# A sorting step beside block-softmax attention: its pieces placed anew over the slots

## What is computed

```
x = x + attn_b(layernorm(x), Wq, Wk, Wv, Wo)        # block softmax, keys in blocks of 64
xf = layernorm(layernorm(x)) * ln_g + ln_b
logits = xf @ router_w                              # [tokens, 8]
scores, idx = top_k(logits, 2); gate = softmax(scores)
out = sum over experts e of gates[:, e] * expert_e(xf)
```

## Time and profile before

| | us |
|---|---|
| median of 3 runs | 2684.78 (2684.75 to 2685.96) |
| profiled execution | 2703.54 |
| its span | 2701.7 |
| PE busy | 2364.6 (88%) |
| DVE busy | 2263.5 (84%) |
| ACT busy | 1622.9 (60%) |
| POOL busy | 1483.6 (55%) |

### The profile page before, as it was taken

How to read it: one execution, slowest core, us unless ns; L and a number is a source line. 1 busy time by engine, 2 the same in 40 slices (tenths; PEclk the granted TensorE clock), 3 DMA queues, 4 the chain that set the end, 5 groups by cost and what they waited for, 6 DMA issues and landing times. The chain is left out here.

```text
span 2701.7 us, 44016 instructions
## 1 busy us (share of the span) xinstructions
PE 2364.6 (88%) x15040; PEld 1796.7 (67%) x15040; DVE 2263.5 (84%) x4665; ACT 1622.9 (60%) x2803; POOL 1483.6 (55%) x1060
## 2 busy tenths in 40 slices
PE   6992179965899999999999999999999999929994
PEld 3552168853677777777777777777777777618883
DVE  5527557757999999999999999999999999737775
...
GB/s 97 157 152 65 42 161 186 195 129 151 110 110 88 102 127 79 98 133 87 69 78 92 68 74 72 87 59 74 84 90 59 74 95 53 14 34 182 189 191 158
DMA packets 171134, 281.22 MB, mean 104 GB/s; under 512 B 32892, under 2 KB 124674, under 8 KB 170912
## 3 DMA queue, kind: packets, MB, share of 16 engines
...
## 5 line engine op out<-in xcount | busy, mean ns | idle before, releaser
L1917 POOL TENSOR_TENSOR b_prob<-b_prob,b_weight 128x1024 f32<-128x1024 f32 x512 | 958.8, 1904 | 514.9 <-DVE b_weight L1877 514.5
L1847 DVE TENSOR_REDUCE b_bmax<-b_score 128x16 f32<-128x1024 f32 x512 | 620.4, 1212 | 38.7 <-PE b_score L1702 24.9
L1800 ACT ACTIVATE b_prob<-b_score,b_neg_m 128x1024 f32<-128x1024 f32 x512 | 582.5, 1138 | 96.1 <-DVE b_neg_m L1855 95.8
L1834 DVE TENSOR_REDUCE b_bsum<-b_prob 128x16 f32<-128x1024 f32 x512 | 605.6, 1202 | 0.0
L1786 ACT ACTIVATE b_pT<-b_turn 128x512 f32<-128x512 f32 x1024 | 561.3, 610 | 60.1 <-PE b_turn L1715 53.3
L1715 PE MATMUL b_turn<-ident,b_prob 128*128 128x128 f32 x4096 | 532.8, 273 | 3.1 <-ACT b_pT L1786 2.8
L1715 PEld LDWEIGHTS b_turn<-ident,b_prob 128*128 128x128 f32 x4096 | 478.7, 141 | 74.4 <-ACT b_pT L1786 3.2
L1702 PE MATMUL b_score<-b_KH,b_QS 128*128 128x512 f32 x1024 | 473.4, 462 | 26.1 <-ACT b_prob L1800 24.9
L1682 PE MATMUL b_acc<-b_pT,b_V 128*64 128x256 f32 x4096 | 470.3, 382 | 0.0
L1702 PE MATMUL b_score<-b_KL,b_QS 128*128 128x512 f32 x1024 | 405.1, 396 | 0.0
L1682 PEld LDWEIGHTS b_acc<-b_pT,b_V 128*64 128x64 f32 x4096 | 282.7, 137 | 151.1 <-issue 21.4
...
...
## 6 DMA issues: line engine op xcount, KB each, us to landing
...
b_KH<-b_k_high SPq DMA_DIRECT2D x128, 256.0 KB
b_KL<-b_k_low SPq DMA_DIRECT2D x128, 256.0 KB
...
```

Of the source, the lines that this page charges most:

```text
L1800: act.activation(prob[r % 4][k][:], score[k % 2][:], ACT.Exp, bias=neg_m[r % 2][:, k:k + 1]).then_inc(prob_ready, 1)
L1834: dve.tensor_reduce(bsum[r % 2][:, k, :], prob[r % 4][k][:].rearrange("p (n c) -> p n c", c=KV_BLOCK), AX, ALU.add).then_inc(sum_ready, 1)
L1847: maxima = chain.mark(dve.tensor_reduce(bmax[r % 2][:, k, :], score[k % 2][:].rearrange("p (n c) -> p n c", c=KV_BLOCK), AX, ALU.max))
L1917: pool.tensor_tensor(tile, tile, weight[r % 2][:, k, :].unsqueeze(2).to_broadcast([P, NB, KV_BLOCK]), ALU.mult).then_inc(scaled, 1)
```

## The change

`LateSort` is split into `Sorter` (the pieces) and `BesideSlots` (their places). It is built with `ways` = 1, so nothing is held twice. The inverse root is made another way: ScalarE takes `Sqrt` of the variance, VectorE its reciprocal, where ScalarE had taken Ln and Exp. What moves:

| piece | engine | `t` before | `t` now |
|---|---|---|---|
| reciprocal, square, fix / rest of the correction | DVE | - and 5 | 5 / 6 |
| normal rows | ACT | 6, 7 | 7, 8 |
| gain, shift | POOL | 8, 9 | 10, 11 |
| second statistics, aggregate, variance | DVE | 10 to 13 | 12 to 15 |
| second root, correction | ACT, DVE | 14, 15 | 16, 17 |
| choice of the two experts | DVE | 19 to 21 | 19 to 21, cut otherwise |
| counts | PE | 21, quarter 2 | 21, quarter 3 |
| places, slots | DVE | 23, 24 | 23, 24, 25 |
| scattering DMAs | POOL | 25 to 30: 3, 3, 2, 3, 3, 2 | 26 to 31: 4, 4, 1, 1, 4, 2 |

VectorE's pieces now stand at the end of quarter 2, but for the copies out of `misc` (logits at `t` 14 and 18, counts at 22), which stay at the end of quarter 0. For sequence 2 the last DMAs are 4, 4, 1, 1, 6.

```diff
-                        if k == PLACE_AT:
+                        if k == 0:
+                            late.vector_takes(dve, sl)
+                        if k == 2:
                             late.vector(dve, chain, sl, wo_taken)
...
-        if t == 8:
...
-        if t == 9:
...
-        if t in (25, 28):
...
-        if 25 <= t < 31:
-            k, third = divmod(t - 25, 3)
...
+        if t == 10:
+            s.pool_gain(pool, n)
+        if t == 11:
+            s.pool_shift(pool, n)
+        if t == 26:
+            s.pool_number(pool, n, 0)
+            s.pool_scatter(pool, n, 0, 0, 4)
+        if t == 27:
+            s.pool_scatter(pool, n, 0, 4, 8)
+        if t == 28:
+            s.pool_number(pool, n, 1)
+            s.pool_scatter(pool, n, 1, 0, 1)
+        if t == 29:
+            s.pool_scatter(pool, n, 1, 1, 2)
+        if t == 30:
+            s.pool_scatter(pool, n, 1, 2, 6 if n + 2 < BATCH else 8)
...
+    def inverse(self, dve, chain, n, which):
...
+        chain.link(dve.reciprocal(self.rstd[:], self.std[:]))
         chain.link(dve.tensor_tensor(self.square[:], self.rstd[:], self.rstd[:], ALU.mult))
         chain.link(dve.tensor_tensor(self.fix[:], self.square[:], self.var[:], ALU.mult))
+    def correct(self, dve, chain):
         chain.link(dve.tensor_scalar(self.square[:], self.fix[:], -0.5, 1.5, ALU.mult, ALU.add))
         chain.link(dve.tensor_tensor(self.rstd[:], self.rstd[:], self.square[:], ALU.mult))
         dve.scalar_tensor_tensor(self.bias[:], self.both[:, :, 0], -1.0, self.rstd[:], ALU.mult, ALU.mult).then_inc(self.biased, 1)
...
+        if t == 5:
+            s.inverse(dve, chain, n, 0)
+        if t == 6:
+            s.correct(dve, chain)
...
+        if t == 17:
+            s.inverse(dve, chain, n, 1)
+            s.correct(dve, chain)
         if t == 19:
+            s.best_of(dve, chain, n)
         if t == 20:
+            s.first_best(dve, chain)
+            s.pick_first(dve, chain)
         if t == 21:
+            s.second_of(dve, chain, n)
+            s.first_best(dve, chain)
+            s.pick_second(dve, chain)
         if t == 23:
+            s.tiles_before(dve, chain, n)
         if t == 24:
+            s.places(dve, chain, n)
+        if t == 25:
+            s.to_slots(dve, chain, n)
```

More of the change, by code:

```diff
@@ L835, in begin, with number, data, normal_rows @@
         self.slot_f = sb("slot_f", [P, 2, TPB])
[L836 to L848, removed]
+        self.slots = [sb(f"slots{i}", [P, 2, TPB], mybir.dt.uint32) for i in range(ways)]
+    LOADS = 5 * 16
+    def number(self, n):
+        return n
+    def data(self, n):
+        return self.rows[n % self.ways][:, :, 0:D]
+    def normal_rows(self, n):
+        return self.hat[:] if self.apart else self.data(n)
+    def loads(self, eng):
+        eng.wait_ge(self.loaded, 48)
     def sync(self, sp):
@@ new lines, in pool_scatter, with pool_end, turn @@
+    def pool_scatter(self, pool, n, k, first, end):
+        for i in range(first, end):
+            pool.indirect_dma_start(out=self.sorted_rows,
+                                    out_offset=bass.IndirectOffsetOnAxis(ap=self.slots[n % self.ways][:, k, i:i + 1], axis=0),
+                                    in_=self.rows[n % self.ways][:, i, :], in_offset=None).then_inc(self.moved, 16)
+    def pool_end(self, pool):
+        pool.wait_ge(self.moved, 32 * TPB * self.number(BATCH - 1))
+    def turn(self, pe, n, half, bank):
+        m = self.number(n)
+        if half == 0:
+            if self.apart:
+                pe.wait_ge(self.normal, m + 1)
+            else:
+                pe.wait_ge(self.xf_ready, m + 1)
+        for i in range(4):
+            last = pe.transpose(bank[:, i * P:(i + 1) * P], self.normal_rows(n)[:, 4 * half + i, :], self.ident[:])
+        last.then_inc(self.turned, 1)
@@ new lines, in scalar_z, with statistics @@
+    def scalar_z(self, act, n, half):
+        m = self.number(n)
+        if half == 0:
+            act.wait_ge(self.biased, 2 * m + 2)
+            if not self.apart:
+                act.wait_ge(self.turned, 2 * m + 2)
+        for i in range(4 * half, 4 * half + 4):
+            row = self.data(n)[:, i, :]
+            last = act.activation(row, row, ACT.Identity, scale=self.rstd[:, i:i + 1], bias=self.bias[:, i:i + 1])
+        if half:
+            last.then_inc(self.z_ready, 1)
+    def statistics(self, dve, chain, n, which, half):
+        if which and half == 0:
+            dve.wait_ge(self.xf_ready, self.number(n) + 1)
+        for i in range(4 * half, 4 * half + 4):
+            src = self.data(n)[:, i, :] if which else self.X[:, n * TPB + i, :]
+            last = dve.bn_stats(self.parts[:, i, :], src)
@@ L1406 @@
 CLEAR_IN = 12
-PLACE_AT = 0
 class Front:
```

390 lines of the change are left out of this document (216 added, 174 removed).

## The result

| | before | after |
|---|---|---|
| median | 2684.93 | 2746.89 |
| lowest to highest of 4 runs each | 2684.75 to 2685.96 | 2745.33 to 2747.46 |
| profiled execution | 2703.54 | 2747.46 |
| its span | 2701.7 | 2745.6 |

After takes 1.0229 times as long as before (95% interval 1.0211 to 1.0247), 62.0 us more; 2720 was predicted. No engine has much more work: this is the page's first part of after (busy time, share of the span, instructions), to be held against the earlier trace rows.

What follows compares the result with a forecast made beforehand. Slots are bound by a loop of weights, GpSimd's weighing and VectorE's scan. Sorting was to cost 25.6 instead of 14.64 a sequence: 11.0 + 11.0 + 13.5 = 35.5 more, 2684.8 + 35.5 = 2720, range 2692 to 2765.

Steps and rivals of the forecast that it cites:

- The sign: Whole kernel: the change was to make it slower, chance 0.81, against 0.14 for faster and 0.05 for same.
- The loop of weights, weighing and scan: Each slot: 12.71 us from one L1877 to the next through GpSimd's weighing and VectorE's scan; four make 50.8 of 51.75.
- the lower bound: Whole kernel: 2693 if 8-column pieces were not held, so that t 5, 6 and 17 cost nothing.
- `t` 8 to 11 and 28 to 31: Slots with `low`: excess to fall from 3.89 to 0.1 and from 2.87 to 1.6.
- The 18.8: Before's median lies this far below its profiled execution; the same step was taken from 2739.0 to reach 2720.
- What was given back: Slot behind a held one: returns what TensorE had kept VectorE waiting, 0.3, 0.8, 0.8 or 0.6 by its place.
- The root: ScalarE's inverse root: Sqrt and the next Exp need two table loads, as Ln and Exp did, so no gain.
- TensorE's clock: Rival, five slots a sequence: half clock after stands costs 1.7 each, 15 times, giving 2745; chance 0.20 shared with lost turns.
- Nothing held: Faster rival, quarter 2: short instructions slip in between GpSimd's reads; a sequence costs 3.9 instead of 14.64, giving 2657; chance 0.14.
- Small pieces not held: Rival, quarter 2: pieces of 8 columns run unheld beside weighings, giving 2690 to 2705; chance 0.11.
- Evened out: Rival, whole kernel: half the holds at the same gains, giving 2685 to 2690; chance 0.05.
- Lost turns: Rival, between weighings: even single pieces wait to +7.6, t 19 reaches 16, giving 2769; chance 0.20 shared with the clock.

Runs made afterwards that it cites:

- e5: After with only one-input pieces in quarter 2, second-half DMAs at t 30 and 31, first inverse and correction at t 7 and 8: 2693.02, 0.9926 of before.
- e3: After with only VectorE's one-input pieces (statistics, aggregates) in quarter 2, all its other pieces in quarter 0: 2665.23, 0.9934 of before.
- e1: After with VectorE's pieces back at the end of quarter 0, the rest of the change kept: 2670.34, 0.9944 of before.
- e4: Before with short linked VectorE instructions added as probes to eight slots without sorting: 2711.82 in one run, 28.1 more than before.
- e6: After with the six VectorE pieces of t = 21 alone back in quarter 0: 2760.90, 1.0181 of before.
- e2: Before with only VectorE's pieces moved to quarter 2 and TensorE's counts to quarter 3: 2759.39, 1.0288 of before.
- e7: After with VectorE's pieces at the end of quarter 3, t = 21 staying in quarter 2: 2754.82, 1.0157 of before.

## Why the prediction was right, and where it was off

**Right, and shown.** The sign and the range (2692 to 2765). The loop of weights, weighing and scan; that a piece with two inputs is held to the end of a weighing, one after another (L1040 to L1042); that pieces of 8 columns are held as well, so the lower bound falls; that `tensor_scalar` is held, which rested on one reading of the earlier trace rows (L1024, alone in `t` 3 and 15, takes 1.11 to 1.13); that statistics are not. `t` 8 to 11 and 28 to 31 came as computed (0.02 for 0.1, 1.79 for 1.6). `t` 24 to 27 came so in sequence 1, 4.84 for 4.8, but not in sequence 0 (6.42). The 18.8 between the profiled execution and the median of before have no counterpart in after, whose profiled execution is within 0.6 of its median. 14.4 of them show as the later start of slot 5, so they came mostly ahead of the slots, and did no harm, as the sum was put on the median. The sum has one slip: four DMAs and the iota are 5.7 against the 5.20 free, so 0.5 over by its own figures and not 0.3; nothing hangs on it.

**Off: 35.5 where 61 to 62 came.** The mechanism was right, and its size was not: the measured loss is 1.75 times the predicted one, still inside the range. 8.5 a sequence are missing. For sequence 0:

- *What was given back*, 0.3 to 0.8 for each slot behind a held one. It is given back where the next slot has no held pieces: `t` 3 and 4 together are 13.60 + 12.74 against 13.18 + 13.18, and `t` = 18 takes 11.94. Where the next slot has pieces of its own, as behind `t` 19, 20 and 23, nothing came back: `t` = 19 costs 0.81 instead of 0, `t` = 20 4.47 instead of 3.5, `t` = 23 2.5 instead of 1.5. This is 2.8 of the 8.5: 1.8 were counted as given back (0.4, 0.6, 0.8), and by 1.0 the holds themselves are longer than the 0.4, 4.1 and 2.3 of the sum.
- *What stays of the old excess.* I replaced the excess of each group by the sum of the holds, but a part of it was never VectorE's two-input pieces: the slot with ScalarE's table loads at `t` = 5 (0.7, by e5), those with the copies out of `misc` at `t` 18 (0.63: 13.24 in e3 and in before) and 22 (0.76). Together 2.1. The sum has only 0.6 of this kind, at `t` 12 to 16.
- *The root*, put at nothing. The first one cost nothing new (`t` 4 to 7 0.72 in e1, 0.81 before). The second did, by its place: with the loads at the head of `t` = 15 before had 13.25 there, 0.06 over its kind; at the head of `t` = 17 e1 and e3 take 13.52 and 13.53, 0.74 over theirs. In after some 0.5 of the 8.5 lie there (`t` 17 and 18 together, less the copy).
- *TensorE's clock.* It was a rival at 25 us, on top of the sum, at 1.7 for each of 15 stands of up to 4 us. The price is right where a fall costs at all (1.75 in e4, 1.64 between e6 and after). The count isn't, nor the length: TensorE stood for 4 us only at `t` = 21 (4.01 in sequence 0, 5.31 in sequence 1), elsewhere for 0.8 to 2.7 at a time. In after a fall shows by itself in `t` = 22 of sequences 0 and 1 (0.56, and 14.91 against 13.37) and in `t` = 18 of sequence 2 (13.56 against 11.95): 3.7 in all. Falls in `t` = 6 of sequence 0 and `t` = 25 of sequences 1 and 2 cost nothing: `t` = 25 takes 12.83 with a fall there, and 12.84 without one in sequence 1 of e6.
- *A lost turn*, in `t` = 25 of sequence 0, which takes 14.69 where sequence 1 takes 12.83; of these 1.86 the next slot gives back 0.3. The windows of `t` = 25, sequences 0 and 1:

```profile
1468.64:1483.34 14.70, 13.17 (x74) 10.36 (x76) 13.49 (x23) 8.89 (x15) 7.75 (x6) 0.77 0.80 188
1918.09:1930.92 12.83, 10.21 (x56) 8.52 (x58) 12.27 (x22) 9.01 (x15) 6.17 (x4) 0.87 0.92 215
```

And its only held piece, the cast L1110, with the weighings of sequence 0, then in sequence 1:

```profile
1475.31 7.49 POOL L2075 TENSOR_TENSOR b_prob<-b_prob,b_weight 128x1024 f32<-128x1024 f32 x4 [8.05 <-DVE b_weight L2033]
...
1479.05 1.91 DVE L1110 CAST b_l_slots<-b_l_slot_f 128x16 uint32<-128x16 f32 x1
```

```profile
1927.85 0.70 DVE L1110 CAST b_l_slots<-b_l_slot_f 128x16 uint32<-128x16 f32 x1
```

In sequence 0 the clock was at 0.50 for 6.8 us of this slot, and the scores of quarter 2 came 0.65 later than in sequence 1. So the cast came up at 1479.05, 0.02 ahead of the end of the second weighing (1479.07), missed its turn, and was held to the end of the third (1480.93), 1.86 more. That a slower clock made it miss is what fits the rows; the missed turn itself is shown.

The rest, about 1 a sequence, is spread over slots at 0.1 to 0.5. That the range held is in part luck: its upper end was drawn for two rivals, and neither came true as written. The clock rival's 2745 lies beside the measured 2747 by accident; its 25 us were 3.7, and the other terms above make up the difference.

**The rivals.** Nothing held: out, by the lengths of L1036 and L1040. Small pieces not held: out, by the same. Evened out: out, by the square of e1 and e2. Lost turns: not as the rule that the rival made of them. `t` = 19, which was to decide, took 13.99 and not 16, and its piece L1063 0.93. Once in after, in the cast above, and nine times in e7 it happened, each time to an instruction that came up at the last moment.

## What to carry to other kernels

Before work is moved into an engine's idle time, ask for each instruction what runs on the other engines in that place: an instruction of VectorE that reads two tiles of SBUF (or a `tensor_scalar`, a copy or a cast between SBUF tiles) cannot be hidden beside GpSimd's `tensor_tensor`, however short it is: it waits to the end of the one that runs. Reductions and statistics can be. A single held piece is mostly given back by the next slot; a chain of them costs one weighing each. It pays to sort the pieces by this one question: e3_split uses the same room and wins where the change loses. And in a sum over slots, write down what stays of the old excess, and count as given back only what falls into a slot that is free.

## What the runs showed of the chip

- *Whose turn it is.* Behind a weighing, an instruction of VectorE that had waited at least 47 ns got in before GpSimd's next instruction, some 700 times in the nine kernels; one that had waited 21 to 40 ns did not, 10 times out of 10 (L1063 and the scan L2013 ahead of a `low` in e7, the cast L1110 in after). Between two `low` it is otherwise: those that had waited 0.16 to 1.04 us lost 36 times, and 60 that had waited 0.65 us or more won. Nothing in the traces says why; it stays open.
- *A fall of TensorE's clock* cost 1.5 to 1.75 us in slots 7 and 27 of e4, in `t` = 18 of after and e6 and in `t` = 22 of sequence 1 of after, 0.56 in one slot and nothing in others. It comes after some stands and not after others of the same length in the same place of the same program; before `t` = 18 the longest was 2.65 us.
- *Equal slots, unequal starts.* The slots agree to 0.1 in all kernels but e4, which has its probes in them, and on both chips (413.88 to 414.00 for the 32 without sorting), but slot 0 begins at 641.88 in after, at 655.37 in before's profiled execution and at 664.72 in e5's. The difference arises ahead of the slots, and not by the program: e7 has after's program there, and its slot 0 begins at 664.49. It is in the main why the spans of before and after understate the difference, and why a profiled execution should be compared slot by slot.
